# Graph layer with pre-norm: ScalarE's queue issues the two halves of adjacency tile 0, SyncE issues x tile 0 and the adjacency from tile 1 on

## The chip, the core and the metric

The kernel runs on one core of a Trainium2 chip. Its engines are TensorE (PE; its weight loads are PEld), VectorE (DVE), ScalarE (ACT), GpSimd (POOL) and SyncE (SP). The metric is the device time of one execution in microseconds (us); less is better. Three runs of the kernel before took 380.98, 381.48 and 381.39 us, median 381.39.

## The reference

With `x` 4096 x 256 and `adj` 4096 x 4096, all float32:

```python
h   = relu(layernorm(x))          # over the 256 features, eps 1e-5
agg = adj @ h
out = x + relu(agg @ W.T + b)
```

## The kernel before

**Precision.** Each float32 product is made of three matmuls in the type fp32r. ScalarE rounds a tile to fp32r (the "hi" part), VectorE subtracts it from the original (the "lo" part), and TensorE adds up hi·hi, h_lo·adj_hi and h_hi·adj_lo in PSUM (`PASSES`).

**Tiles.** The transposed adjacency is cut into 4 groups of 1024 output columns, and each group into 32 tiles of 128 x 1024 (0.5 MB), tile t holding the rows p·32+t. A ring of `U = 4` buffers `adj_in[:, k, :]` takes the tiles in turn. A tile gives 12 matmuls of 512 columns (line 401): 3 passes, 2 feature blocks, 2 column chunks of 512. The first `EARLY = 2` tiles are loaded in two halves of 128 x 512 (256 KB each, one semaphore `s_early[t][c]` for each half), so that work can start on a half. Below, "half (t, c)" is column chunk c of tile t.

**Start of the program.** SP issues x tile 0 (128 KB), then the halves (0,0), (0,1), (1,0), (1,1), then whole tiles from 2 on (line 164; from tile 4 on it waits until the buffer is free). POOL issues x tiles 1, 2 and 3, and later pieces of four x tiles. VectorE takes mean and variance of x tile 0 (lines 238 to 254), POOL raises the variance to the power -0.5 (line 202), ScalarE writes the rounded h (line 344) and then rounds the halves (line 338). The order on ScalarE is

```python
h_rounded(0)
early_rounded(0, 0)
early_rounded(0, 1)
h_rounded(1)
early_rounded(1, 0)
early_rounded(1, 1)
```

and from tile 2 on `adj_rounded(t)` (line 334), then `h_rounded(t)`. TensorE first runs 10 warm-up matmuls on constants (`WARM_UP`), waits for half (0,0) to land, runs 3 short ones (`WARM_ON`, 256 columns), and then `early_tile(0)`: 4 matmuls on half (0,0) (hi and h_lo), 4 on half (0,1), then 4 with adj_lo. So the fifth real matmul is the first that needs half (0,1).

**The rest.** Each group ends with the product with W (line 443), placed in the next group's tile stream. [...]

Of the kernel before, what the change touches and what calls it, by code (L numbers as in the profile page):

```python
# [7 lines left out]
def bass_preln_gnn_residual(  # L8
# [21 lines left out]
    CHUNKS = 2  # L30
# [16 lines left out]
    adj_v = adj_t.rearrange("(p t) i -> p t i", t=TILES)  # L47
# [5 lines left out]
    with ctx:  # L53
        def sb(name, shape, dt=fp32):
            return ctx.enter_context(nc.sbuf_tensor(name, shape, dt))

        def sem(name):
            return ctx.enter_context(nc.semaphore(name))
# [7 lines left out]
        adj_in = sb("adj_in", [P, U, GW])  # L66
# [23 lines left out]
        s_early = [[sem(f"adj{t}_chunk{c}_landed") for c in range(CHUNKS)] for t in range(EARLY)]  # L90
# [26 lines left out]
        def bank(g, block_, c):  # L117
            return banks[(g % 2) * SUMS + c * KB + block_]
# [3 lines left out]
        def chunk(c):  # L122
            return slice(c * BANK, (c + 1) * BANK)
# [8 lines left out]
        def made_tile(n):  # L132
            return made_chunk(n, CHUNKS - 1) if n < EARLY else CHUNKS * EARLY + n - EARLY + 1

        def pieces(g):

            whole = [(c, o, 0, BANK) for c, o in GROUP_BANKS]
            if g < LAST:
                return whole
            c, o, _, _ = whole.pop()  # L140
            return whole + [(c, o, 0, BANK // 2), (c, o, BANK // 2, BANK)]

        def within(c, a, b):
            return slice(c * BANK + a, c * BANK + b)

        def product(g, c, o, a, b):

            return bank(g if a == 0 else g + 1, o, c)[:, a:b]

        def load_x(engine, i):  # L150
            a, b = X_PIECES[i]
            engine.dma_start(x_sb[:, a:b, :], x_v[:, a:b, :]).then_inc(s_x[i], 16)  # L152

        @block.sync
        def _(sp):
            def load_chunk(t, c):
                sp.dma_start(adj_in[:, t, chunk(c)], adj_v[:, t, chunk(c)]).then_inc(s_early[t][c], 16)

            def load_adj(n):
                g, t = divmod(n, TILES)  # L160
                if n >= U:
                    sp.wait_ge(s_hi, made_tile(n - U))
                    sp.wait_ge(s_lo, made_tile(n - U))
                sp.dma_start(adj_in[:, n % U, :], adj_v[:, t, g * GW:(g + 1) * GW]).then_inc(s_adj[n % U], 16)


            load_x(sp, 0)
            load_chunk(0, 0)
            load_chunk(0, 1)
            load_chunk(1, 0)  # L170
            load_chunk(1, 1)
            for n in range(EARLY, GROUPS * TILES):
                load_adj(n)

            sp.wait_ge(s_out, 16 * LAST)
            for i, (c, o, a, b) in enumerate(pieces(LAST)):
                sp.wait_ge(s_sum, LAST * SUMS + i + 1)
                at = LAST * GW + c * BANK
                sp.dma_start(out_v[:, o, at + a:at + b], out_sb[:, o, within(c, a, b)]).then_inc(s_last[i], 16)
            for s in s_last:  # L180
                sp.wait_ge(s, 16)

        @block.gpsimd
        def _(pool):
            for i in range(1, U):
                load_x(pool, i)
# [18 lines left out]
            for t in range(TILES):  # L205
                root(t)
                if t == 0:
                    load_x(pool, U)
                i = t // U + U + 1
                if t % U == 2 and i < len(X_PIECES):  # L210
                    load_x(pool, i)
                if t == 7:
                    pool.dma_start(w_sb[:], wt_v).then_inc(s_w, 16)
                    pool.dma_start(b_sb[:], b_cols).then_inc(s_b, 16)
# [111 lines left out]
        @block.scalar  # L326
        def _(act):
            def adj_rounded(n):
                k = n % U

                act.wait_ge(s_adj[k], 16 * (n // U + (k >= EARLY)))
                if n >= U:
                    act.wait_ge(s_pe, n - U + 1)
                nc.scalar.activation(adj_hi[:, k, :], adj_in[:, k, :], ACT.Copy).then_inc(s_hi, 1)  # L334

            def early_rounded(t, c):
                act.wait_ge(s_early[t][c], 16)
                nc.scalar.activation(adj_hi[:, t, chunk(c)], adj_in[:, t, chunk(c)], ACT.Copy).then_inc(s_hi, 1)  # L338

            def h_rounded(t):  # L340
                k = t % U
                act.wait_ge(s_rstd, t + 1)
                act.wait_ge(s_centred, t + 1)
                nc.scalar.activation(h_sb[:, t, 0, :], centred[:, k, :], ACT.Copy,  # L344
                                     scale=rstd[:, k:k + 1]).then_inc(s_hhi, 1)


            nc.scalar.activation(scratch[:], nc.const_aps.tensor(1.0, [P, 1], fp32), ACT.Copy)
            h_rounded(0)
# [5 lines that stand above are left out]
            for t in range(EARLY, TILES):  # L355
                adj_rounded(t)
                h_rounded(t)

            act.wait_ge(s_w, 16)
            nc.scalar.activation(w_hi[:], w_sb[:], ACT.Copy).then_inc(s_whi, 1)  # L360

            def sums_rounded(g):
                if g >= 1:
                    act.wait_ge(s_prod, g * SUMS)
                if g < LAST:
                    act.wait_ge(s_pe, (g + 1) * TILES)
                for i, (c, kb) in enumerate(GROUP_BANKS):
                    if g == LAST:
                        act.wait_ge(s_chunk, c + 1)
                    nc.scalar.activation(agg_hi[:, kb, chunk(c)], bank(g, kb, c)[:], ACT.Copy  # L370
                                         ).then_inc(s_ahi, 1)

            def add_bias(g):

                act.wait_ge(s_xt, 16 * (g + 1))
                for c, o in GROUP_BANKS:
                    nc.scalar.activation(xt_sb[:, o, chunk(c)], xt_sb[:, o, chunk(c)],  # L377
                                         ACT.Identity, bias=b_sb[:, o:o + 1]).then_inc(s_xb, 1)

            act.wait_ge(s_b, 16)  # L380
            for g in range(1, GROUPS):
                for t in range(TILES):
                    if t == SPLIT_AT:
                        sums_rounded(g - 1)
                    if t == OUT_AT:
                        add_bias(g - 1)
                    adj_rounded(g * TILES + t)
            add_bias(LAST)
            sums_rounded(LAST)
# [115 lines left out]
```

## Time and profile before

| | us |
|---|---|
| median of 3 runs (380.98 to 381.48) | 381.39 |
| the profiled execution | 381.01 |
| its span, first to last instruction | 379.2 |
| PE busy in the span | 375.4 |
| DVE, ACT, POOL busy | 216.5, 169.0, 62.8 |

The page gives each engine's busy time in the span, and the chain of work that ended last. Matmuls are pipelined: a matmul of 512 columns is shown with about 0.39 us, though the next one starts about 0.23 us after it, so the step between two is read from starts, and rows that merge several matmuls give it as (length of the row − length of one) / (count − 1). In the rows of the DMA issues the last number is the time from the start of the issue to the landing of all its data.

### The profile page before, as it was taken

The page shows a single profiled execution, that of the slowest core. Times are in us where ns is not written, and L with a number is a line of the kernel's source. Part 1 is how long each engine was busy: PE and PEld are TensorE (multiplying, and loading weights), DVE is VectorE, ACT ScalarE, POOL GpSimd, SP SyncE. Part 2 cuts the span into 40 slices and gives each one's busy share as a digit, 9 for nine tenths or more (in the row PEclk, how much of TensorE's full clock was granted, in tenths as well). Part 3 has the DMA queues.
Part 4 walks back from the last instruction along what each step waited for, and adds up shares of the span by engine and source line. Part 5 has one row for each costly group of instructions (what it writes and reads, how often), then busy time and mean ns, then how long its engine had stood idle before and what let it go on. Part 6 is the DMA issues. An engine that isn't in the chain of part 4 may idle for free.

```text
span 379.2 us, 4427 instructions
## 1 busy us (share of the span) xinstructions
PE 375.4 (99%) x1651; PEld 308.2 (81%) x1651; DVE 216.5 (57%) x294; ACT 169.0 (45%) x197; POOL 62.8 (17%) x88
## 2 busy tenths in 40 slices
PE   8999999999999999999999999999999999999997
PEld 4888888888888888888888888888888888888885
DVE  5999999884745353535564444444464444444424
ACT  5666564654543434343643343433355243434341
POOL 5587777550010000000001000000000100000000
PEclk9999999999999999999999999999999999999999
DMA  7998887668659565656566856555666775566203
GB/s 269 353 305 271 275 279 264 187 209 287 205 185 322 178 209 178 208 180 208 175 208 204 292 184 204 182 198 191 197 193 189 256 243 200 186 203 186 90 2 111
DMA packets 22774, 80.25 MB, mean 212 GB/s; under 512 B 2496, under 2 KB 2880, under 8 KB 22752
## 3 DMA queue, kind: packets, MB, share of 16 engines
q1 hardware_dynamic: 19584, 68.30, 54.8%
q0 software_dynamic: 3168, 11.67, 8.5%
q8 instruction: 13, 0.21, 0.2%
q14 instruction: 9, 0.07, 0.0%
HBM read 75.76 MB, written 4.19 MB: 211 GB/s over the span
## 4 chain that ended last, share of the span: by engine, by line
PE 98%; DMA 1%; ACT 0%; DVE 0%; SPq 0%; issue 0%
PE bank L401 92%; PE bank L443 6%; DMA adj_in<-adj_t_dram 1%; ACT adj_hi L338 0%; DVE out_sb L312 0%; SPq L152 0%
## 5 line engine op out<-in xcount | busy, mean ns | idle before, releaser
L401 PE MATMUL bank<-adj_hi,h_sb 128*128 128x512 f32 x1024 | 254.4, 389 | 0.2 <-ACT adj_hi L338 0.2
L227 DVE TENSOR_TENSOR adj_lo<-adj_in,adj_hi 128x1024 fp32r<-128x1024 f32 x126 | 153.9, 1221 | 142.9 <-ACT adj_hi L334 142.9
L401 PEld LDWEIGHTS bank<-adj_hi,h_sb 128*128 128x128 f32 x1024 | 192.0, 188 | 40.5 <-issue 0.4
L334 ACT ACTIVATE adj_hi<-adj_in 128x1024 fp32r<-128x1024 f32 x126 | 133.5, 1060 | 180.7 <-PE bank L401 177.3
L401 PE MATMUL bank<-adj_lo,h_sb 128*128 128x512 f32 x512 | 137.5, 389 | 0.0
L401 PEld LDWEIGHTS bank<-adj_lo,h_sb 128*128 128x128 f32 x512 | 96.1, 188 | 20.0
L219 POOL DMA_DIRECT2D out_t_dram<-out_sb x3 | 2.2, 727 | 209.7 <-DVE out_sb L312 209.7
L202 POOL TENSOR_TENSOR rstd<-var_eps,minus_half 128x1 f32<-128x1 f32 x32 | 27.9, 871 | 3.1 <-DVE var_eps L247 0.7
L196 POOL TENSOR_TENSOR var_eps<-mean_var,eps_sb 128x1 f32<-128x1 f32 x31 | 22.7, 732 | 20.7 <-DVE mean_var L243 20.3
L344 ACT ACTIVATE h_sb<-centred,rstd 128x256 fp32r<-128x256 f32 x32 | 16.1, 502 | 15.0 <-POOL rstd L202 15.0
L260 DVE SCALAR_TENSOR_TENSOR h_sb<-centred,rstd,h_sb 128x256 fp32r<-128x256 f32 x32 | 15.3, 478 | 1.0 <-ACT h_sb L344 1.0
L238 DVE BATCH_NORM_STATS2 stats<-x_sb 128x6 f32<-128x256 f32 x32 | 13.5, 420 | 2.8 <-DMA x_sb<-x_dram 2.8
L301 DVE TENSOR_TENSOR agg_lo<-bank,agg_hi 128x512 fp32r<-128x512 f32 x16 | 10.0, 683 | 7.8 <-ACT agg_hi L370 7.8
L312 DVE SCALAR_TENSOR_TENSOR out_sb<-bank,minus_b,xt_sb 128x512 f32<-128x512 f32 (+1 forms) x17 | 11.4, 715 | 4.7 <-ACT xt_sb L377 3.7
L254 DVE TENSOR_SCALAR centred<-x_sb,mean_var 128x256 f32<-128x256 f32 x32 | 13.1, 410 | 0.0
L443 PE MATMUL bank<-agg_lo,w_hi 128*128 128x512 f32 (+1 forms) x34 | 12.8, 376 | 0.0
L443 PE MATMUL bank<-agg_hi,w_lo 128*128 128x512 f32 (+1 forms) x34 | 12.8, 376 | 0.0
L443 PE MATMUL bank<-agg_hi,w_hi 128*128 128x512 f32 (+1 forms) x34 | 12.8, 376 | 0.0
L370 ACT ACTIVATE agg_hi<-bank 128x512 fp32r<-128x512 f32 x16 | 8.3, 596 | 6.2 <-PE bank L401 6.2
L377 ACT ACTIVATE xt_sb<-xt_sb,b_sb 128x512 f32<-128x512 f32 x16 | 10.2, 708 | 0.0
L443 PEld LDWEIGHTS bank<-agg_hi,w_hi 128*128 128x128 f32 x34 | 6.4, 188 | 1.2
L443 PEld LDWEIGHTS bank<-agg_lo,w_hi 128*128 128x128 f32 x34 | 6.4, 188 | 1.2
(23 smaller groups left out, 37.8 us busy)
## 6 DMA issues: line engine op xcount, KB each, us to landing
adj_in<-adj_t_dram SPq DMA_DIRECT2D x126, 512.0 KB, 3.7
xt_sb<-x_t_dram POOLq DMA_DIRECT2D x4, 1024.0 KB, 7.7
x_sb<-x_dram POOLq DMA_DIRECT2D x7, 512.0 KB, 6.1
out_t_dram<-out_sb POOLq DMA_DIRECT2D x3, 1024.0 KB, 4.9
adj_in<-adj_t_dram SPq DMA_DIRECT2D x4, 256.0 KB, 4.8
out_t_dram<-out_sb SPq DMA_DIRECT2D x3, 256.0 KB, 2.1
x_sb<-x_dram POOLq DMA_DIRECT2D x3, 128.0 KB, 4.9
w_sb<-w_t_dram POOLq DMA_DIRECT2D x1, 256.0 KB, 4.8
```

Source lines behind the costliest of these rows:

```text
L196: nc.gpsimd.tensor_tensor(var_eps[:, k:k + 1], mean_var[:, k, 1:2], eps_sb[:], ALU.add).then_inc(s_var, 1)
L202: nc.gpsimd.tensor_tensor(rstd[:, k:k + 1], var_eps[:, k:k + 1], minus_half[:], ALU.pow).then_inc(s_rstd, 1)
L227: nc.vector.tensor_tensor(adj_lo[:, k, :], adj_in[:, k, :], adj_hi[:, k, :].bitcast(fp32), ALU.subtract).then_inc(s_lo, 1)
L238: nc.vector.bn_stats(stats[:, k, :], x_sb[:, t, :]).then_inc(s_stats, 1)
L254: nc.vector.tensor_scalar(centred[:, k, :], x_sb[:, t, :], mean_var[:, k, 0:1], mean_var[:, k, 0:1], ALU.max, ALU.subtract).then_inc(s_cen ...
L260: nc.vector.scalar_tensor_tensor(out=h_sb[:, t, 1, :], in0=centred[:, k, :], scalar=rstd[:, k:k + 1], in1=h_sb[:, t, 0, :].bitcast(fp32), ...
L312: nc.vector.scalar_tensor_tensor(out=out_sb[:, o, cols], in0=product(g, c, o, a, b), scalar=minus_b[:, o:o + 1], in1=xt_sb[:, o, cols], op ...
L334: nc.scalar.activation(adj_hi[:, k, :], adj_in[:, k, :], ACT.Copy).then_inc(s_hi, 1)
L344: nc.scalar.activation(h_sb[:, t, 0, :], centred[:, k, :], ACT.Copy, scale=rstd[:, k:k + 1]).then_inc(s_hhi, 1)
L377: nc.scalar.activation(xt_sb[:, o, chunk(c)], xt_sb[:, o, chunk(c)], ACT.Identity, bias=b_sb[:, o:o + 1]).then_inc(s_xb, 1)
L401: last = nc.tensor.matmul(bank(g, kb, c)[:], h_sb[:, t, hp, kb * P:(kb + 1) * P], adj_parts[ap][:, n % U, chunk(c)], start=(t == 0 and (hp ...
L443: last = nc.tensor.matmul(product(g, c, o, a, b), (w_hi, w_lo)[wp][:, kb, o * P:(o + 1) * P], (agg_hi, agg_lo)[ap][:, kb, within(c, a, b)] ...
```

## The change

ScalarE's instruction stream now begins with the two issues of tile 0's halves, ahead of its table load. SP issues x tile 0, the two halves of tile 1, and then the whole tiles as before. Nothing else is changed; each transfer raises the semaphore that it raised before.

```diff
+        def load_chunk(engine, t, c):
+            engine.dma_start(adj_in[:, t, chunk(c)], adj_v[:, t, chunk(c)]).then_inc(s_early[t][c], 16)
...
         @block.sync
         def _(sp):
-            def load_chunk(t, c):
-                sp.dma_start(adj_in[:, t, chunk(c)], adj_v[:, t, chunk(c)]).then_inc(s_early[t][c], 16)
-
...
             load_x(sp, 0)
-            load_chunk(0, 0)
-            load_chunk(0, 1)
-            load_chunk(1, 0)
-            load_chunk(1, 1)
+            for c in range(CHUNKS):
+                load_chunk(sp, 1, c)
             for n in range(EARLY, GROUPS * TILES):
                 load_adj(n)
...
+            for c in range(CHUNKS):
+                load_chunk(act, 0, c)
 
             nc.scalar.activation(scratch[:], nc.const_aps.tensor(1.0, [P, 1], fp32), ACT.Copy)
             h_rounded(0)
```

ScalarE's first instructions before (line 344 is the rounded h, line 338 the rounding of a half):

```order
L326 UNCONDITIONAL_BRANCH
L348 ACT_TABLE_LOAD
L348 ACTIVATE scratch<-const-float32-1.0 128x1
L344 ACTIVATE h_sb<-centred,rstd 128x256
L338 ACTIVATE adj_hi<-adj_in 128x512 x2
```

and now:

```order
L324 UNCONDITIONAL_BRANCH
L151 DMA adj_in<-adj_t_dram 128x512 x2
L348 ACT_TABLE_LOAD
L348 ACTIVATE scratch<-const-float32-1.0 128x1
L342 ACTIVATE h_sb<-centred,rstd 128x256
L336 ACTIVATE adj_hi<-adj_in 128x512 x2
```

The two issues stand ahead of the table load and of everything that ScalarE computes. SP's whole program before (line 152 is x tile 0, 157 the halves, 164 the whole tiles, 179 the stores of the last group):

```order
L154 UNCONDITIONAL_BRANCH
L152 DMA x_sb<-x_dram 128x256
L157 DMA adj_in<-adj_t_dram 128x512 x4
L164 DMA adj_in<-adj_t_dram 128x1024 x126
L179 DMA out_t_dram<-out_sb 128x512 x3
```

and now:

```order
L157 UNCONDITIONAL_BRANCH
L155 DMA x_sb<-x_dram 128x256
L151 DMA adj_in<-adj_t_dram 128x512 x2
L164 DMA adj_in<-adj_t_dram 128x1024 x126
L177 DMA out_t_dram<-out_sb 128x512 x3
```

SP issues two transfers fewer ahead of tile 1's halves and of tile 2. The instructions of TensorE, VectorE and POOL keep their order.

## Rows read from the trace of the kernel before

**Rows 1.** The page, busy time and chain of waits.
```profile
PE 375.4 (99%) x1651; PEld 308.2 (81%) x1651; DVE 216.5 (57%) x294; ACT 169.0 (45%) x197; POOL 62.8 (17%) x88
...
PE 98%; DMA 1%; ACT 0%; DVE 0%; SPq 0%; issue 0%
```

**Rows 2.** The chain that ended last: start us, length us, what.
```profile
1.18 3.93 DMA adj_in<-adj_t_dram
...
5.13 0.64 ACT adj_hi L338
...
5.91 98.40 PE bank L401 x432
```

**Rows 3.** The timeline of ACT, 4 to 12: start, length [idle before, releaser].
```profile
4.45 0.51 ACT L344 ACTIVATE h_sb<-centred,rstd 128x256 fp32r<-128x256 f32 x1 [2.21 <-POOL rstd L202]
5.13 0.63 ACT L338 ACTIVATE adj_hi<-adj_in 128x512 fp32r<-128x512 f32 x1 [0.18 <-DMA adj_in<-adj_t_dram]
5.95 0.63 ACT L338 ACTIVATE adj_hi<-adj_in 128x512 fp32r<-128x512 f32 x1 [0.19 <-DMA adj_in<-adj_t_dram]
...
7.80 1.25 ACT L338 ACTIVATE adj_hi<-adj_in 128x512 fp32r<-128x512 f32 x2
10.02 1.06 ACT L334 ACTIVATE adj_hi<-adj_in 128x1024 fp32r<-128x1024 f32 x1 [0.97 <-DMA adj_in<-adj_t_dram]
10.99 0.49 ACT L344 ACTIVATE h_sb<-centred,rstd 128x256 fp32r<-128x256 f32 x1
```

**Rows 4.** The timeline of PE: 4 to 4.4, 5.1, 5.9 to 6.95, 8.7 to 9.7, 11.2 to 11.9.
```profile
3.72 1.06 PE L456 MATMUL bank<-const-bfloat16-1.0 128*128 128x512 bf16 x2
...
4.57 0.63 PE L456 MATMUL bank<-const-bfloat16-1.0 128*128 128x512 bf16 x1
...
5.91 1.39 PE L401 MATMUL bank<-adj_hi,h_sb 128*128 128x512 f32 x5 [0.19 <-ACT adj_hi L338]
...
8.74 1.32 PE L401 MATMUL bank<-adj_hi,h_sb 128*128 128x512 f32 x5
...
10.83 0.84 PE L401 MATMUL bank<-adj_lo,h_sb 128*128 128x512 f32 x3
11.53 0.73 PE L401 MATMUL bank<-adj_hi,h_sb 128*128 128x512 f32 x2
```

**Rows 5.** The timeline of ACT and DVE up to the first use of x.
```profile
0.74 1.28 ACT L348 ACT_TABLE_LOAD   x1 [0.74 <-PEq L498]
2.03 0.20 ACT L348 ACTIVATE scratch<-const-float32-1.0 128x1 f32<-128x1 f32 x1
...
2.84 0.43 DVE L238 BATCH_NORM_STATS2 stats<-x_sb 128x6 f32<-128x256 f32 x1 [2.84 <-DMA x_sb<-x_dram]
```

**Rows 6.** The timeline of the DMA issues of SP and POOL, 1.18 to 3.07.
```profile
1.18 1.85 SPq L157 DMA_DIRECT2D adj_in<-adj_t_dram  x4
1.25 1.77 POOL L152 DMA_DIRECT2D x_sb<-x_dram  x3 [0.81 <-POOLq L498]
```

**Rows 7.** DMA issues in 1.6 to 1.7 and 3.0 to 3.3: count, KB, us to landing.
```profile
adj_in<-adj_t_dram SPq DMA_DIRECT2D x1, 256.0 KB, 4.3
x_sb<-x_dram POOLq DMA_DIRECT2D x1, 128.0 KB, 4.1
...
adj_in<-adj_t_dram SPq DMA_DIRECT2D x1, 512.0 KB, 6.9
```

**Rows 8.** DMA traffic, 1.7 to 2.4, 2.4 to 3.8, 3.8 to 5.8.
```profile
q1 hardware_dynamic: 141, 0.13, 64.4%
...
q1 hardware_dynamic: 80, 0.15, 40.4%
...
DMA packets 362, 0.75 MB, mean 376 GB/s; under 512 B 55, under 2 KB 55, under 8 KB 362
...
q1 hardware_dynamic: 278, 0.51, 66.2%
q0 software_dynamic: 84, 0.25, 37.5%
```

## The prediction

> **What bounds the kernel now.** I read the page first, then the chain of waits, then the timelines of the first 14 us, since the change touches nothing later. The page gives PE 99% of the span, and the chain is PE for 98% of it [rows 1]. In the chain the reader sees one unbroken stretch of matmuls from 5.91 us to the end, and ahead of it half (0,0)'s transfer (1.18 to 5.11) and ScalarE's rounding of it at 5.13 [rows 2]. So two things alone can move the end: when PE starts (5.91), and how much PE is held up in its first tiles. The first 432 matmuls take 98.40 us; the later steps between them are (1.39 − 0.39) / 4 = 0.25 in the first row and 0.23 afterwards [rows 2, 4], so all hold-ups together are some 0.5 us.
>
> There are four deadlines in the stretch:
> - Start. ScalarE ends h tile 0 at 4.45 + 0.51 = 4.96 and half (0,0) is there at 1.18 + 3.93 = 5.11 [rows 2, 3]. It rounds from 5.13 to 5.76, and PE starts 0.15 later. The transfer is late by 0.15 only; behind it stands the h chain, which hangs on x tile 0 (VectorE starts on it at 2.84 [rows 5]).
> - Half (0,1). It lands 4.3 after its issue, at about 5.93; ScalarE rounds it from 5.95 to 6.58 [rows 3, 7]. PE could use it at 6.58 + 0.15 = 6.73. Its fifth matmul, the first to need it, starts at 5.91 + 1.39 − 0.39 = 6.91 [rows 4]. So it has 0.18 to spare: a landing after 6.11 stops PE.
> - Tile 1. ScalarE has its first half rounded at 7.80 + 0.63 = 8.43, usable at 8.58, and PE takes it at 8.74 [rows 3, 4]: 0.16 to spare.
> - Tile 2. It lands at 3.07 + 6.9, about 10.0; ScalarE rounds it at 10.02, then makes h tile 2 until 11.48, and PE's first matmul on it is at 11.53 [rows 3, 4, 7]. Without a wait PE would be there at 10.83 + 3 × 0.227 = 11.51, and the second matmul starts at 11.53 + 0.73 − 0.39 = 11.87 where 11.74 would do: 0.13 to 0.15 is lost here. I take 0.13. A delay of PE ahead of this point is repaid up to 0.13, if tile 2 comes no later.
>
> **The change part by part.**
> - Two issues less on SP. Four take 1.85, so one takes 0.46 [rows 6]: tile 1's halves and tile 2 are issued 0.92 sooner. From 3.8 us on the DMA engines are the limit (376 GB/s, shares of 66.2% and 37.5% [rows 8]), so an earlier issue helps only by what is moved earlier. Tile 2 comes no later than now, by my estimate 0.2 to 0.4 sooner: its hold-up of 0.13 goes.
> - Two issues more on ScalarE. The bounds are SP's 0.46 and POOL's, whose issues take longer (1.77 for three, 0.59 each [rows 6]). The table load then starts at 0.74 + 2 × 0.46 = 1.66 (1.92 at the upper bound), ends 1.28 later, and the scratch instruction ends at 3.15 (3.40). ScalarE's first work comes at 4.45 [rows 3, 5]. More than 1 us of idle time hides all of it. Cost 0.
> - The trace has the scratch instruction at 2.03, right behind the load's end at 2.02 [rows 5]. [...]
> - Half (0,0) is issued at 0.74 and not at 1.18: 0.44 sooner. Its first packets come after x tile 0's: in the stretch 1.7 to 2.4 all 141 packets are x tile 0's 1 KB rows and their semaphores, and the adjacency begins after 2.4 [rows 8]. Started 0.44 sooner, it meets the last third of x tile 0. x tile 0 can lose from 0 up to 0.6 (its eight rows on each of 16 engines, each behind an adjacency row; such a row takes 0.662 × 2.0 / (278 / 16) = 0.076 [rows 8]); I take 0.15, since most of x is through by then. Then h tile 0 ends at 5.11, and PE starts at 5.11 + 0.02 + 0.63 + 0.15 = 5.91, as now. With nothing lost it would start at 5.76, and not sooner, however early the half lands: a ceiling of 0.15 on this part.
> - Half (0,1) is what I expect to be late. Now the halves are served one after another from one queue. In the changed kernel (0,0) and (0,1) stand in ScalarE's queue, and (1,0), (1,1) and tile 2 in SP's beside it, with POOL's x tiles as a third. If the DMA engines take turns, tile 0 gets half of what it gets now. Do they take turns? From 3.8 to 5.8 q1 (SP) moves 0.51 MB in 2 KB rows and q0 (POOL) 0.25 MB in 1 KB rows while both are backed up [rows 8]: as many rows of each. That is what turns by row would give. With rows of 2, 2 and 1 KB, ScalarE's queue gets 2/5 of 376, or 150 GB/s.
>
> The sum for half (0,1) goes like this. At present the adjacency moves only 0.15 MB from 2.4 to 3.8 with engines 40% busy [rows 8]: a slow start not limited by the engines. After it, 0.37 of tile 0's 0.52 MB remain; at 0.51 / 2.0 = 255 GB/s these are through at 3.8 + 1.45 = 5.25, and the last engine's share has landed at 5.93, so a lag of 0.68. Afterwards the slow start ends at 3.8 − 0.44 = 3.36. If it runs for both queues side by side, 0.37 MB at 150 GB/s take 2.47: 3.36 + 2.47 + 0.68 = 6.5. If both queues share the slow start, 0.45 MB remain and take 3.0: 7.05. If ScalarE's queue were served as SP's is now, it would be 3.36 + 1.45 + 0.68 = 5.5. I take 6.75, between the first two. It is late by 6.75 − 6.11 = 0.64. Tile 2 gives back 0.13. The rest is +0.5 us.
>
> [...]
>
> - Tile 1 hangs on x tile 1 too, which lands 4.1 after POOL's issue at 1.25, at 5.35 [rows 6, 7]. With three queues POOL's share falls from 1/3 to 1/5, so x tile 1 may be 0.3 to 0.6 late. Its slack is 0.16 plus PE's own 0.64, so 0.8: nothing added.
>
> Sum: start 0, half (0,1) +0.64, tile 2 −0.13, so +0.5 us. On the profiled execution's 381.01 that is 381.5; that execution lies 0.38 under the median of 381.39, and on the median it would be 381.9. The three runs spread over 0.5; I take 381.8, a little toward the profiled execution on which the sum rests. The difference counts as 0.2% (0.76 us), about the least that a measurement of this kernel tells from no change; +0.5 lies inside.
>
> **The rivals.**
> 1. ScalarE's queue keeps its lead (its data asked for 0.44 sooner is served first, SP's queue gets what is over). Half (0,1) lands at about 5.5, x tile 0 loses nothing: −0.15 for the start, −0.13 at tile 2, 381.1. For it: the head start, and engines only 40% busy in the slow start. Against it: q0 and q1 plainly share. No change by the bound, and the most that this edit can gain.
> 2. Even turns, and a slow start that the two queues share: half (0,1) at 7.05 or later. [...] It decides from a landing at 6.11 + 0.13 + 0.76 = 7.0 on. For it: 0.15 MB in 1.4 us looks like a limit outside the queues, in the adjacency's reads themselves. Against it: rows of tile 1 may find that start-up cost paid by tile 0.
> 3. x tile 0 is held up by half (0,0) in full. A delay of 0.6 gives PE's start at 5.76 + 0.6 = 6.36, and +0.45 − 0.13 = +0.3 by itself; over 0.76 it is only from a delay of 1.04 on, since 0.15 + 0.13 are spare. For it: both are issued at 0.74. Against it: all of x was through by 2.4, and the adjacency, issued at 1.18, sent nothing before that. Price at a delay of 1.2: +0.9, 382.3.
> [...]
>
> **Chances.** The forecast (half (0,1) between 6.3 and 7.0) 0.50; rival 1 and what lies between it and the forecast 0.22; rival 2 0.17; rival 3 at a price over the bound 0.07; rival 4 or something in the other direction of the same kind 0.04. Faster by over 0.2% needs a gain of 0.76, and all parts together have 0.28: 0.02. Slower is rivals 2, 3, most of 4: 0.26. Within 0.2%: 0.72. The range goes from rival 1 less 0.2 for the spread of the runs (380.9) to rival 2 with some more (382.9).
>
> **What would show it.** In the changed profile: ScalarE's issues at 0.74 and 1.2, table load at about 1.66, without effect on h tile 0. ScalarE's second rounding of a half, now at 5.95, begins at about 6.8 with a wait for the DMA, and PE shows a gap ahead of its fifth real matmul. PE starts between 5.76 and 6.1. The gap before tile 2's first matmuls is gone. If the second rounding begins before 6.1, the even sharing is wrong and rival 1 holds; if VectorE starts on x tile 0 after 3.3, rival 3 does. The forecast as a whole is wrong if the time leaves 380.9 to 382.9.

## The result and the profile after

The changed kernel takes 382.15 us, median of 14 runs (381.90 to 383.29), against 381.05 us for the kernel before (14 runs, 380.73 to 381.67): ratio 1.0033, 95% interval 1.0025 to 1.0040. It is slower by 1.1 us at the medians and by 1.26 by the ratio, more than the 0.2% that counts as a difference here. The 14 runs fall into two groups: ten at 381.90 to 382.25, middle 381.97, and four at 383.16 to 383.29. The profiled execution took 383.20 us and is of the second group. So there are 0.92 us to explain in the first group (381.97 − 381.05), and 383.20 − 381.01 = 2.19 in the profile.

The page of the changed kernel, busy time (1) and DMA queues (3):

```profile
PE 376.9 (99%) x1651; PEld 309.5 (81%) x1651; DVE 216.6 (57%) x294; ACT 168.6 (44%) x197; POOL 62.9 (16%) x88
...
q1 hardware_dynamic: 19296, 67.77, 53.9%
q0 software_dynamic: 3168, 11.67, 8.4%
q10 hardware_dynamic: 288, 0.52, 0.5%
```

ScalarE's two transfers have a queue of their own, q10: 288 packets, 0.52 MB. The number of instructions is the same. The chain of the changed kernel that ended last (start, length, what):

```profile
0.74 3.27 DMA x_sb<-x_dram
...
4.03 0.44 DVE stats L236
...
5.02 0.59 POOL rstd L200
...
5.64 0.51 ACT h_sb L342
6.14 0.53 ACT adj_hi L336
6.67 0.14 issue
6.81 99.72 PE bank L401 x432
```

In the chain before, half (0,0)'s transfer stood ahead of PE [rows 2]. Now it is x tile 0's: used at 4.03 and not at 2.84 [rows 5]. ScalarE's h tile 0 comes 1.19 later with it (5.64 for 4.45), and PE starts at 6.81 and not at 5.91, so +0.90. The first 432 matmuls take 99.72 and not 98.40, so +1.32. Together 2.22, which is the profile's difference of 2.19 to within 0.03. The timelines of ACT and PE show both parts:

```profile
1.66 1.28 ACT L348 ACT_TABLE_LOAD   x1 [1.66 <-PEq L498]
2.95 0.20 ACT L348 ACTIVATE scratch<-const-float32-1.0 128x1 f32<-128x1 f32 x1
...
5.64 0.51 ACT L342 ACTIVATE h_sb<-centred,rstd 128x256 fp32r<-128x256 f32 x1 [2.48 <-POOL rstd L200]
6.05 1.13 ACT L336 ACTIVATE adj_hi<-adj_in 128x512 fp32r<-128x512 f32 x2
```

```profile
6.81 3.56 PE L401 MATMUL bank<-adj_hi,h_sb 128*128 128x512 f32 x8 [0.97 <-ACT adj_hi L336]
10.21 1.09 PE L401 MATMUL bank<-adj_lo,h_sb 128*128 128x512 f32 x4
```

The table load at 1.66 has no effect: ScalarE then waits 2.48 us for POOL. Its two roundings of tile 0's halves follow each other without a wait, so half (0,1) is not late for anybody. And the first eight real matmuls take (10.21 − 6.81) / 8 = 0.425 us each, the step of the warm-ups of 512 columns (1.06 − 0.63 = 0.43 [rows 4]); only then comes the 0.23 of [rows 4]. Below, these two are the slow and the quick step. The granted clock in this profile stands at 1.00 from 0 us on, for the slow warm-ups as well, so here the steps have to tell it. The 13 warm-up matmuls had taken until 5.85, which their slow step accounts for (10 × 0.43 + 3 × 0.21 = 4.9 of the 5.07; 0.21 is the step of the short ones, which start at 5.00 and 5.21):

```profile
0.78 5.07 PE L456 MATMUL bank<-const-bfloat16-1.0 128*128 128x512 bf16 x13 [0.78 <-PEq L498]
```

DMA traffic of the changed kernel from 1.7 to 2.4 and from 1.7 to 3.8 (packets, MB, share of 16 engines):

```profile
q1 hardware_dynamic: 58, 0.06, 35.5%
q10 hardware_dynamic: 20, 0.04, 27.9%
...
q10 hardware_dynamic: 143, 0.26, 50.5%
q1 hardware_dynamic: 162, 0.17, 41.2%
```

Before, q1 moved all of x tile 0 by 2.4 (141 packets [rows 8]); now 58. An adjacency row of q10 took 0.505 × 2.1 × 16 / 143 = 0.119 us on the mean of the longer stretch, and 0.279 × 0.7 × 16 / 20 = 0.156 in the shorter one, beside x tile 0.

### The profile page after: what moved, and what is told of

It reads as the page before. It is cut to its first block, busy times and chain, and to the rows that moved or that the text cites. A ratio compares the mean times of both kernels' runs of the same rounds, so it can differ in the third digit from the quotient of the medians.

```text
span 381.4 us, 4427 instructions
## 1 busy us (share of the span) xinstructions
PE 376.9 (99%) x1651; PEld 309.5 (81%) x1651; DVE 216.6 (57%) x294; ACT 168.6 (44%) x197; POOL 62.9 (16%) x88
## 4 chain that ended last, share of the span: by engine, by line
PE 97%; DMA 1%; DVE 0%; ACT 0%; POOL 0%; issue 0%; POOLq 0%
PE bank L401 92%; PE bank L443 6%; DMA x_sb<-x_dram 1%; POOL rstd L200 0%; ACT adj_hi L336 0%; ACT h_sb L342 0%; DVE out_sb L310 0%; DVE stats L236 0%; DVE mean_var L241 0%; DVE var_eps L245 0%; POOLq L196 0%
## 5 line engine op out<-in xcount | busy, mean ns | idle before, releaser
L200 POOL TENSOR_TENSOR rstd<-var_eps,minus_half 128x1 f32<-128x1 f32 x32 | 29.7, 928 | 4.3 <-DVE var_eps L245 1.9
L194 POOL TENSOR_TENSOR var_eps<-mean_var,eps_sb 128x1 f32<-128x1 f32 x31 | 20.9, 674 | 21.6 <-DVE mean_var L241 21.3
```

The costliest lines, as they stand in the source:

```text
L194: nc.gpsimd.tensor_tensor(var_eps[:, k:k + 1], mean_var[:, k, 1:2], eps_sb[:], ALU.add).then_inc(s_var, 1)
L200: nc.gpsimd.tensor_tensor(rstd[:, k:k + 1], var_eps[:, k:k + 1], minus_half[:], ALU.pow).then_inc(s_rstd, 1)
```

## Experiments

Eleven kernels, one of them run twice, tell the causes apart. The start of VectorE's moments of x tile 0 and of PE's first real matmul are from each kernel's profile. "Late h, n" is the kernel before with n extra VectorE instructions ahead of these moments. Differences are to the runs of the kernel before on the same chips, 380.91 to 381.03.

| kernel | x tile 0 used | PE starts | median us (runs) | ratio, 95% |
|---|---|---|---|---|
| before | 2.84 | 5.91 | 381.05 (14) | |
| changed | 4.03 | 6.81 | 382.15 (14) | 1.0033 (1.0025 to 1.0040) |
| e1 late h, 3 | 3.47 | 6.23 | 381.35 (11) | 1.0011 (1.0002 to 1.0020) |
| e5 late h, 6 | 4.12 | 6.90 | 381.96 (12) | 1.0025 (1.0015 to 1.0035) |
| e6 late h, 6, 12 warm-ups | 4.08 | 6.84 | 381.95 (11) | 1.0021 (1.0012 to 1.0030) |
| e2 changed, 12 warm-ups | 4.06 | 6.84 | 381.91 (9) | 1.0028 (1.0018 to 1.0038) |
| e4 x tile 0 on ACT | 4.44 | 7.23 | 383.73 (5) | 1.0073 (1.0061 to 1.0086) |
| e8 half (0,1) alone on ACT | 3.88 | 6.66 | 381.61 (12) | 1.0015 (1.0005 to 1.0025) |
| e7 x tile 1 on ACT | 3.26 | 6.23 | 381.73 (12) | 1.0023 (1.0007 to 1.0038) |
| e10 x tile 1 on SP | 2.78 | 6.65 | 381.71 (9) | 1.0033 (1.0018 to 1.0048) |
| e3 ACT's issues behind its first work | 3.06 | 5.83 | 382.07 (7) | 1.0028 (1.0018 to 1.0039) |
| e9 e3, x tile 1 on SP | 3.78 | 6.56 | 380.93 (11) | 0.9996 (0.9988 to 1.0005) |
| e11 e9 again | 2.90 | 5.68 | 380.88 (11) | 0.9999 (0.9991 to 1.0008) |
| e12 e9, x tile 2 on SP too | 3.69 | 6.46 | 380.84 (11) | 0.9996 (0.9987 to 1.0005) |

In e7, e9 and e12 the profiled execution was the slowest of its kernel (384.38, 381.62 and 381.59), so their first two columns are not those of the median.

### Is it the late use of x tile 0? (e1, e5)

```diff
+            pad = sb("pad", [P, 3, D])
+            dve.wait_ge(s_x[0], 16)
+            for j in range(3):
+                nc.vector.tensor_scalar(pad[:, j, :], x_sb[:, 0, :], 1.0, None, ALU.mult)
             moments(0)
```

> The kernel before, with three extra VectorE instructions (each like the 0.40 us centring of one x tile, writing to a tile nobody reads) ahead of the moments of x tile 0. All transfers stay as before. Theory A (the loss of the change is that the h chain of tile 0 starts 1.2 us later, whatever the transfers do): VectorE's moments start at about 2.84 + 1.2 = 4.04, PE's first real matmul at about 6.8 to 6.95, time +0.8 to +1.0 us over the kernel before in the faster group of runs, and some runs 1.1 us longer still, because TensorE idles from about 5.6 to 6.8. Rival B (the loss comes from the order in which the adjacency halves land or from general DMA contention): this kernel loses less than 0.3 us.

The three instructions delayed the moments by 0.63 only, about half of what the centring's 0.40 each had promised, so the sizes fit neither side, and six were taken (e5).

> The kernel before with six extra VectorE instructions ahead of the moments of x tile 0 (three of them delayed the moments by only 0.63 us, to 3.47, and cost 0.4 us). Theory A (the loss of the change is x tile 0's late use, and nothing else of the transfers matters): the moments start at about 4.05 to 4.1 as in the changed kernel (4.03), PE starts at 6.8 to 6.9, and the runs lie in the changed kernel's two groups, about 381.9 and about 383.2 us. Rival B (a good part of the changed kernel's loss is the late landing of x tile 1 and half (0,1)): this kernel stays at least 0.3 us under the changed one, below 381.7.

The timelines of DVE and PE in e5:

```profile
2.91 1.30 DVE L268 TENSOR_SCALAR pad<-x_sb 128x256 f32<-128x256 f32 x6 [2.91 <-DMA x_sb<-x_dram]
4.12 0.42 DVE L238 BATCH_NORM_STATS2 stats<-x_sb 128x6 f32<-128x256 f32 x1
```

```profile
6.90 2.08 PE L405 MATMUL bank<-adj_hi,h_sb 128*128 128x512 f32 x8 [1.56 <-ACT adj_hi L342]
```

And that of ACT:

```profile
5.73 0.51 ACT L348 ACTIVATE h_sb<-centred,rstd 128x256 fp32r<-128x256 f32 x1 [3.49 <-POOL rstd L202]
6.14 1.14 ACT L342 ACTIVATE adj_hi<-adj_in 128x512 fp32r<-128x512 f32 x2
```

With all transfers as before and x tile 0 used at 4.12, the time is 381.96; ten runs lie at 381.89 to 382.10 and two at 383.3, the changed kernel's two groups. Theory A holds. The two delays also give the slack. 0.63 costs 381.35 − 380.96 = 0.39, 1.28 costs 381.96 − 380.97 = 0.99: each is the delay less 0.24 to 0.29. The prediction had 0.15 to spare at the start and 0.13 at tile 2. The changed kernel's 1.19 less 0.28 is 0.91, and its first group shows 0.92.

Where the slack lies, the chains of e1 (first line) and e5 tell:

```profile
6.23 98.43 PE bank L405 x432
```

```profile
6.90 98.39 PE bank L405 x432
```

PE starts 0.32 and 0.99 later than at 5.91, for delays of 0.63 and 1.28. So all of the slack, 0.29 to 0.31, is at the start, and the 432 matmuls take what they took before (98.40 [rows 2]): no hold-up is given back on balance.

### What makes the second group? (e2, e6)

```diff
-    WARM_UP = 10
+    WARM_UP = 12
```

> The changed kernel with 12 warm-up matmuls of 512 columns in place of 10. Theory A (of the profiled 2.2 us, 1.3 to 1.5 is eight matmuls at the slow clock, because TensorE idled 1.16 us between the warm-ups and the first real matmul at 6.81, and in 4 of 14 executions the clock then rises only at about 10 us): the warm-ups last until about 6.5, the group of runs at 383.2 us is gone and all lie at 381.9 to 382.3; PE still starts at about 6.8. Rival B (the late rise has nothing to do with the idle gap, only with when the program starts): some runs at 383.2 us stay.

e6 makes the same edit to e5:

> The same delay of x tile 0's use by six VectorE instructions, with 12 warm-up matmuls in place of 10. Theory A (the slower group of runs is the clock that rises late after an idle TensorE): all runs lie in the faster group, 381.8 to 382.3 us, none at 383. Rival B (the group is the phase of the clock alone): the slower group appears here as often as with 10 warm-ups.

None of the 9 runs of e2 (highest 382.70) and none of the 11 of e6 (highest 382.05) was in the upper group. With 10 warm-ups 4 of 14 and 2 of 12 were. Of 6 such runs among 46 none falls among these 20 by luck in 1 case of 40, so this speaks for theory A without settling it. In e2's and e6's profiles PE idled for 1.38 and 1.39 all the same, since the warm-ups had changed to a quicker step before they ended (15 of them in 4.69 us in e2 and 4.67 in e6, where the changed kernel's profile has 13 in 5.07; from 4.0 to 5.0 e2 has six of them and the changed kernel three). The idle time was not closed. Its length alone does not make the group either: behind 1.38, 1.39 and 1.56 (e5) the first 432 matmuls took 98.39, 98.41 and 98.39 in these profiles, behind 0.97 in the changed kernel's 99.72. Nor do slow warm-ups alone: in e1 and e9 the 13 took 5.06, and behind gaps of 0.39 and 0.72 the first eight real matmuls had steps of 0.25 and 0.24. The changed kernel is 0.95 above the kernel before with 12 warm-ups, and 1.10 with 10.

### Which transfer holds up x tile 0? (e4, e8, e7)

e4 exchanges the roles:

```diff
-            load_x(sp, 0)
+            for c in range(CHUNKS):
+                load_chunk(sp, 0, c)
             for c in range(CHUNKS):
                 load_chunk(sp, 1, c)
...
-            for c in range(CHUNKS):
-                load_chunk(act, 0, c)
+            load_x(act, 0)
```

> The queues' roles exchanged: ScalarE issues x tile 0 as its first work at 0.74, SP issues all four halves in the order (0,0), (0,1), (1,0), (1,1) from 0.74 and then the whole tiles, so there is no second queue of adjacency. Theory A (rows of half (0,0) and of x tile 0 take turns on the 16 DMA engines and x waits behind the slow first adjacency rows): x tile 0 is again used at about 3.7 to 4.1, PE starts at 6.5 to 6.9, +0.7 to +1.1 us over the kernel before. Rival B (it is the two adjacency streams side by side that slow x tile 0, through the tile 1 halves on SP's queue): x tile 0 is used before 3.3 and the time is within 0.3 us of the kernel before.

Theory A, and worse than it said: x tile 0 is used at 4.44. One adjacency queue beside x is enough. All five runs took 383.6 to 383.9. The timeline of PE in e4, and its windows (busy, granted clock, DMA share, GB/s):

```profile
7.23 3.27 PE L401 MATMUL bank<-adj_hi,h_sb 128*128 128x512 f32 x8 [2.03 <-ACT adj_hi L337]
10.29 1.52 PE L401 MATMUL bank<-adj_lo,h_sb 128*128 128x512 f32 x4
```

```profile
7.23:7.80 0.57, 0.57 (x3) 1.00 1.08 424
7.80:11.20 3.40, 3.40 (x10) 0.50 1.00 369
11.20:14.00 2.80, 2.80 (x14) 1.00 0.78 237
```

After 2.03 us without work TensorE still has a granted clock of 1.00 for 0.57 us, then 0.50 from 7.80 to 11.20, then 1.00 again. The cost is of the second group's kind and size, but the course is another: here the 13 warm-ups took 4.42 us, six of them in 4.0 to 5.0, so the quick step had come before the gap and was lost behind it, while in the changed kernel's profile the warm-ups (13 in 5.07) and the first eight matmuls all had the slow step. In e4 it is 0.425 too (two steps from 8.16 to 9.01); 3.4 us hold eight such steps where fifteen quick ones would fit, so about 1.6 us are lost. With the start (7.23 − 5.91 = 1.32) less the 0.13 of tile 2, which slow matmuls do give back, this makes 2.8; measured is 383.73 − 380.96 = 2.77. In the profile of the changed kernel eight steps at 0.425 and not 0.23 likewise make 1.56, of which hold-ups that are gone give back 0.24.

e8 leaves only half (0,1) to ScalarE:

```diff
             load_x(sp, 0)
+            load_chunk(sp, 0, 0)
...
-            for c in range(CHUNKS):
-                load_chunk(act, 0, c)
+            load_chunk(act, 0, 1)
```

> ScalarE issues only half (0,1) at 0.74; SP issues x tile 0, then (0,0), (1,0), (1,1). Theory A (one adjacency half in flight beside x tile 0 is enough): x tile 0 is used at 3.7 to 4.1, as in the changed kernel, time +0.8 to +1.2 us. Rival B (the delay grows with what is queued): x tile 0 is used at 3.2 to 3.5 and the time rises by 0.3 to 0.5 us.

In e8 x tile 0 is used at 3.88 (theory A's place), and the time is +0.64, between the two expectations. In e7 ScalarE issues x tile 1 instead, from the kernel before:

```diff
-            for i in range(1, U):
+            for i in range(2, U):
                 load_x(pool, i)
...
+            load_x(act, 1)
             nc.scalar.activation(scratch[:], nc.const_aps.tensor(1.0, [P, 1], fp32), ACT.Copy)
```

> The kernel before, with one transfer moved: x tile 1 (128 KB in 1 KB rows) is issued by ScalarE as its first work at 0.74 and not by POOL at 1.25. SP's queue is as before. Theory A (what holds x tile 0 up in the changed kernel is the slow start of the first adjacency rows, behind which its rows wait): x tile 0 is used at 2.85 to 3.2, x tile 1 lands at 3 to 3.5, time within 0.3 us of the kernel before, on either side. Rival B (any second hardware queue at that moment costs x tile 0 about 1 us): x tile 0 is used at 3.5 or later and the time rises by 0.5 us or more.

The first use of x tile 0 by DVE, in e8 and in e7:

```profile
3.88 0.43 DVE L237 BATCH_NORM_STATS2 stats<-x_sb 128x6 f32<-128x256 f32 x1 [3.88 <-DMA x_sb<-x_dram]
```

```profile
3.26 0.43 DVE L238 BATCH_NORM_STATS2 stats<-x_sb 128x6 f32<-128x256 f32 x1 [3.26 <-DMA x_sb<-x_dram]
```

128 KB of 1 KB x rows in the second queue delay x tile 0 by 0.42, adjacency rows by 1.0 to 1.6. So a second queue with x rows alone was not free in e7, and the rest goes with adjacency rows in it. That is near theory A for the landing (3.26 for its 2.85 to 3.2). That it is the slowness of these rows is argued from their price; they are also twice as long, and the transfer twice as large, and no run separates the three. For the time neither holds: +0.76 at the median, with runs from 381.18 to 384.38. Its profile is of the 384.38 run:

```profile
8.34 0.63 ACT L338 ACTIVATE adj_hi<-adj_in 128x512 fp32r<-128x512 f32 x1 [2.26 <-DMA adj_in<-adj_t_dram]
```

Half (0,1) is rounded only at 8.34, PE waits 1.63 us for it, and the granted clock is 0.50 from 9.03 to 11.9. So the time of that run has a second cause, the late half; why it was late is open.

### What if ScalarE issues later? (e3, e9, e11, e12, e10)

```diff
-            for c in range(CHUNKS):
-                load_chunk(act, 0, c)
...
             nc.scalar.activation(scratch[:], nc.const_aps.tensor(1.0, [P, 1], fp32), ACT.Copy)
+            for c in range(CHUNKS):
+                load_chunk(act, 0, c)
```

> The changed kernel with ScalarE's two issues moved behind its table load and the scratch instruction (issued at about 2.25 and 2.7 us, when x tile 0 is nearly through). Theory A (x tile 0 is held up only because half (0,0) is asked for at the same time): x tile 0 is used at 2.84 to 3.0, not at 4.03; but SP's tile 1 halves (issued from 1.18) run first, half (0,0) lands at 5.0 to 6.0, PE starts at 5.9 to 6.8, time between the two kernels or like the changed one. Rival B (any second hardware queue slows x tile 0, or ScalarE's queue is slow by itself): x tile 0 is used after 3.5.

The timeline of ACT in e3:

```profile
0.74 1.28 ACT L346 ACT_TABLE_LOAD   x1 [0.74 <-PEq L498]
0.80 0.86 ACTq L151 DMA_DIRECT2D adj_in<-adj_t_dram  x2
2.04 0.20 ACT L346 ACTIVATE scratch<-const-float32-1.0 128x1 f32<-128x1 f32 x1
```

The premise was wrong: the issues, written behind the load and the scratch instruction, went out at 0.80 and not at 2.25, while the load ran. They come 0.06 later than in the changed kernel, and yet x tile 0 is used at 3.06. In the stretch 1.7 to 2.2, q1 now has 72 packets through and q10 none (first row); in the changed kernel 41 and 7:

```profile
q1 hardware_dynamic: 72, 0.07, 69.5%
```

```profile
q1 hardware_dynamic: 41, 0.04, 38.7%
q10 hardware_dynamic: 7, 0.01, 17.9%
```

So the start of q10's rows, 0.06 us of issue time apart, goes with x tile 0's landing here. It does not decide it: e9 below issues at 0.80 too, and its profile has the same count in 1.7 to 2.2 and none of q10. Yet x tile 0 is used there at 3.78:

```profile
q1 hardware_dynamic: 72, 0.07, 56.2%
```

In e3 PE starts at 5.83, sooner than before. But the time is no better than the changed kernel's. The timeline of PE in e3, and of ACT:

```profile
5.83 2.41 PE L401 MATMUL bank<-adj_hi,h_sb 128*128 128x512 f32 x8 [0.29 <-ACT adj_hi L336]
...
9.95 1.39 PE L401 MATMUL bank<-adj_hi,h_sb 128*128 128x512 f32 x5 [0.24 <-ACT adj_hi L336]
```

```profile
6.37 0.63 ACT L336 ACTIVATE adj_hi<-adj_in 128x512 fp32r<-128x512 f32 x1 [0.68 <-DMA adj_in<-adj_t_dram]
8.78 0.51 ACT L342 ACTIVATE h_sb<-centred,rstd 128x256 fp32r<-128x256 f32 x1 [1.77 <-POOL rstd L200]
```

Half (0,1) is waited for (0.68), as the prediction had it, and tile 1 starts at 9.95 where it was 8.74 [rows 4]: h tile 1 is made at 8.78, since POOL's x tile 1 is late: VectorE waits for it until 6.77, as late as in the changed kernel. e9, made from e3, gives x tile 1 to SP:

```diff
             load_x(sp, 0)
+            load_x(sp, 1)
...
-            for i in range(1, U):
+            for i in range(2, U):
                 load_x(pool, i)
```

> As the kernel in which ScalarE issues tile 0's halves behind its scratch instruction, and x tile 1 issued by SP right behind x tile 0 in place of POOL. Theory A (that kernel, which started PE at 5.83, lost its 1.1 us because x tile 1 landed at 6.75 and h tile 1 came at 8.78): x tile 1 lands at 3.2 to 4.0, h tile 1 is made before 7.8, no PE gap ahead of tile 1, and the time is within 0.3 us of the kernel before. Rival B (the loss is half (0,1), which landed at 6.35, and tile 0's other matmuls): the time stays 0.7 us or more over the kernel before.

> The same kernel as the one with tile 0's halves issued late by ScalarE and x tile 1 by SP, run again for a second interval and a profile from the middle of its runs (the first profile was of its slowest, with x tile 0 used at 3.78). Theory A: 380.8 to 381.1 us again, no difference to the kernel before; x tile 0 used at 2.8 to 3.1, PE starts at 5.75 to 5.95, no gap ahead of tile 1. Rival B: it is faster than the kernel before by 0.1 us or more beyond its interval.

The timeline of PE in e11:

```profile
5.68 2.08 PE L402 MATMUL bank<-adj_hi,h_sb 128*128 128x512 f32 x8 [0.54 <-ACT adj_hi L337]
7.60 1.08 PE L402 MATMUL bank<-adj_lo,h_sb 128*128 128x512 f32 x4
8.62 2.06 PE L402 MATMUL bank<-adj_hi,h_sb 128*128 128x512 f32 x8
```

Tile 1 starts at 8.62 and the 1.1 us are gone: 380.93 and 380.88, no difference to the kernel before in either run. The edit also lets half (0,1) land sooner (at 5.6 in e11, 6.35 in e3), so the time alone does not tell the two apart; e3's timeline does, since the rounding of tile 1 follows h tile 1 there. e12 moves x tile 2 in the same way and stays there (380.84):

> As that kernel, with x tile 2 issued by SP too, behind x tile 1. Theory A (x tiles in one queue behind x tile 0 do not disturb it, and tile 1's halves come about 0.3 later without being missed): 380.8 to 381.2 us. Rival B (the later halves of tile 1 now hold up PE ahead of tile 1 or 2): 381.4 us or more.

e10 is the kernel before with x tile 1 behind x tile 0 on SP, ScalarE issuing nothing:

> The kernel before with x tile 1 issued by SP, right behind x tile 0 and ahead of the halves; POOL issues x tiles 2 and 3. One hardware queue, as before. Theory A (only a second queue disturbs x tile 0): x tile 0 is used at 2.8 to 2.9; half (0,0) is issued 0.46 later, lands at 5.2 to 5.6, PE starts 0.1 to 0.5 later, time +0.1 to +0.5 us, less where x tile 1 out of POOL's queue speeds up the halves. Rival B (x tile 0's landing depends on the whole traffic behind it): x tile 0 is used at 3.1 or later.

x tile 0 is used at 2.78 (2.84 before), so in this profile the traffic queued behind it did not hold it up; half (0,0) is late, PE starts at 6.65, and the median is +0.68, more than the 0.5 expected, with four of nine runs at 382.9 to 383.6.

## Why the prediction came out as it did

The time lay in the range and the sign of the forecast was right, but the forecast's mechanism was not what happened. It was +0.5 from half (0,1); measured is +1.1, from x tile 0. That 381.8 came so near to 382.15 is luck: the median before was taken as 381.39 from three runs, and 14 give 381.05, so 0.34 of the nearness is the starting value. And a difference within 0.2% had been given 0.72; the measured 1.0033 is the outcome "slower", which had 0.26.

- **x tile 0, the step that failed.** The prediction took 0.15 from a range of 0 to 0.6. Measured: 1.19. Two things were wrong in it. The price of a turn was read from the quick stretch (0.076 us a row in 3.8 to 5.8), though x tile 0 meets the adjacency in its slow start, where the same rows show 0.404 × 1.4 × 16 / 80 = 0.113 [rows 8]; the changed kernel shows 0.119. Eight turns are then 0.9 to 0.95 and not 0.6, and with the 0.156 of 1.7 to 2.4 itself 1.25. That each x row waits for one adjacency row is the author's estimate and was not shown: by 2.4 q1 had 58 packets through and q10 20. And "most of x is through by then" came from sliding the adjacency's first row to 2.11 over a stream of x that would itself run on undisturbed; it did not (58 packets of q1 by 2.4, not 141). e5 shows that this delay alone gives the time.
- **The start.** The sum of the two slacks, 0.28, was right, its parts were not. The prediction let the rounding begin 0.02 behind the end of h tile 0. In e5 ScalarE begins it 0.41 after the start of h tile 0 (6.14 for 5.73), before that instruction's 0.51 are over, and PE starts 1.17 after the start of h tile 0 where it was 1.46 before. So 0.29 is to spare at the start, and e11 starts PE at 5.68, under the ceiling of 5.76. The 0.13 of tile 2 is no gain: in e5 it goes (the first eight matmuls of tile 2 take 14.46 − 12.65 = 1.81, before 13.48 − 11.53 = 1.95), and tile 1 is held up by 0.11 instead (9.84 − 8.82 = 1.02, before 8.74 − 7.83 = 0.91). Rival 3, priced at a delay of 1.2 with +0.9 and 382.3, is what happened, and its sign came (VectorE on x tile 0 after 3.3); it had been given a chance of 0.07.
- **Half (0,1).** It was the main term, late by 0.64. In the changed kernel's profile it landed at 6.43 for the forecast 6.75 (in e2's at 5.87), PE's fifth matmul comes at 8.51 for 6.91 before, and half (0,1) is rounded without a wait: the term is hidden behind the larger one. Where x tile 0 was in time (e3) the wait showed, at 6.37 for an expected 6.77. In 3.8 to 5.8 of the changed kernel SP's and ScalarE's queues do share nearly evenly:

```profile
q1 hardware_dynamic: 160, 0.30, 41.1%
q10 hardware_dynamic: 138, 0.26, 33.2%
```

So the sharing was right, its price too high by 0.3, and it was not decisive. The upper end of the range was taken from rival 2 with half (0,1) beyond 7.05; no run shows the two queues side by side lengthening the slow start: by 3.8 q10 alone had 0.26 MB through, where the adjacency had 0.15 before [rows 8], and the half was there at 6.43.
- **x tile 1.** It was to be 0.3 to 0.6 late behind a slack of 0.8. It landed 5.5 after POOL's issue at 1.25 and not 4.1 [rows 7], so 1.4 late, in the changed kernel and in e3. In e3, where PE was not late, it cost the most, and e9 took it away.
- **ScalarE's issues.** 0.89 us for both, no effect, as predicted.
- **The clock (rival 4).** Its share of the chances was at most 0.04. In the changed kernel's profile a start that is late for another reason leaves TensorE idle for 0.97, and the first eight real matmuls then have a step of 0.425; 4 of 14 runs took 1.2 us more than the others. That the idle time is what makes the step slow was the author's estimate: e2, e6 and e5 had longer gaps (1.38 to 1.56) and steps of 0.24. This is the part of the median (0.18 of 1.10) that rival 3 did not have.

What stays open: why x tile 0 was late in the profiles of e9 and e12 (3.78, 3.69), the slowest executions of kernels whose other runs were not slow; only that it can happen with the issue at 0.80 is shown. The other 31 of the 33 runs of e9, e11 and e12 lie at 380.74 to 381.18. e7's spread is open as well, and so is what decides whether an idle gap costs the slow matmuls or not.

## What to carry to other kernels

In the changed kernel x tile 0 headed the longest chain. Where nothing but its rows and their semaphores went through the DMA engines from 1.7 to 2.4 (141 packets [rows 8]), it was used at 2.84; with 20 packets of q10 among them and 58 of q1, at 4.03. Before a second queue is opened beside such a transfer, even for the next thing needed, look at what it does to it: here it cost 0.42 to 1.60 us (e7, e4). With ScalarE's issue 0.06 us later it cost 0.06 and 0.22 in two profiles (e11, e3) and 0.94 and 0.85 in two others (e9, e12), the only two of the 33 runs of e9, e11 and e12 above 381.18. Price such a clash by the duration of rows in that very stretch (0.113 us here), not in a later one (0.076). And look at how long a late first matmul leaves TensorE idle: behind gaps of 0.97 (changed) and 2.03 (e4) the first 432 matmuls took 1.3 and 1.4 us more than before, on top of starts 0.90 and 1.32 late, though behind 1.38 to 1.56 (e2, e6, e5) they took what they took before (98.39 to 98.41 for 98.40).

## What the runs showed of the hardware

- A DMA issue written behind a table load and an activation went out at 0.80, during the load (0.74 to 2.02), in e3, e9, e11 and e12; written ahead of the load it held the load back to 1.66. So the order as written did not hold the issue back until the compute ahead of it was done.
- The first adjacency rows were slow: 0.113 us in 2.4 to 3.8 against 0.076 for the same 2 KB in 3.8 to 5.8, with the engines 40.4% busy with this queue [rows 8]. In the changed kernel x tile 0 beside them was through later: 58 of q1's packets in 1.7 to 2.4 and not 141.
- With the same issue at 0.80 x tile 0 was used at 3.06, 2.90, 3.78 and 3.69 in four profiles (e3, e11, e9, e12).
- TensorE's clock was granted at 1.00 for 0.57 us after an idle gap of 2.03, then at 0.50 for 3.4 us while it was working without a pause (e4). In the changed kernel's profile eight matmuls ran at 0.425 a step behind slow warm-ups (13 in 5.07) and a gap of 0.97, with the granted clock shown at 1.00.
- Two ScalarE instructions back to back overlapped: the rounding began 0.41 after the start of h tile 0, which is shown with 0.51 (e5; the same in the changed kernel, 6.05 for 5.64).
- The extra VectorE instructions took 1.21 / 6 = 0.20 us each (2.91 to 4.12), half of the centring's 0.40 on the same 128 x 256 shape.
